# A graph layer and its experts: products and low parts by blocks of columns, one-hots with a scalar operand, high parts behind both layers

## The chip, the cores and the metric

The kernel runs on one core of a Trainium2 chip. The time is the device time of one execution in microseconds (us), as the median of three runs. Every number of the profile comes from one further, profiled execution.

## The reference

x is 6250 rows of 256 numbers, with 100,000 edges sorted by their target dst. Layernorm is LN(x). The kernel computes

```
h    = LN(x);  r = relation_emb[edge_type];  gate = sigmoid(r @ gate_w.T + gate_b)
m    = (clifford(h[src] * r, msg_w, msg_b)) * gate * (deg_src[src] * deg_dst[dst]) ** -0.5
x    = x + clifford(h + segment_sum(m, dst), upd_w, upd_b)
w    = softmax(mean(LN(x)) @ Wr + br)          # per row here: the leading axis has length 1
x    = x + sum over 8 experts e of w[:, e] * (relu(bn2(relu(bn1(LN(x) @ W1[e])) @ W2[e])) @ Wo[e] + bo[e])
```

where clifford is a 256x256 matrix put together from four 64x64 parts.

## The kernel before

Edges come in blocks of 128 (one a partition), four blocks to a superblock; there are 196 superblocks. Rows of x come in 49 tiles of 128, in 27 groups of one or two tiles (22 have two). A group of two tiles uses up 8 superblocks.

*A superblock J.* GpSimd gathers its four blocks of 260 columns of the scaled h table into H (L440, one indirect DMA a block; a ring of 6 superblocks), and the relation rows of two or three of the blocks into R. The other one or two blocks' relation rows are read by TensorE instead: ScalarE makes a one-hot of the edge type (L571, L574) and TensorE multiplies it with the relation table into PSUM (`rel_pe`, L885). VectorE then makes the products in place: H times R over all gathered blocks in one instruction (L1287, 520 or 780 columns; 1040 in the last superblocks) and H times PSUM for each block that was read (L1291, 258 columns). Columns 256 and 257 carry the norm and a one; columns 258 and 259 are padding.

TensorE sums the products over the edges of a target by a one-hot S of the edge's place in its tile. It does so in a reduced format, and so each product is split: ScalarE makes the high part HI (`high_act`, L583, 1040 columns), VectorE the low part LO = H - HI (`low_dve`, L1304, 1040 columns) and S for four blocks in one instruction (L1300, two broadcast operands). TensorE multiplies S with HI and LO (`sb_pe`, L873). VectorE takes the sums out of PSUM for each two superblocks (`take_dve`, L1262, L1266).

*A group g* runs its experts in ten stages s0 to s9 (`ffn` of each engine). In stage s TensorE does layer w1 of expert s, layer w2 of expert s-1 (both L825) and the output y of expert s-2 (L857); ScalarE the two relus (L632) into h1 and h2; VectorE adds y into acc (L1238). So s8 has no w1, s9 only y, s0 only w1. At the end of a stage comes its hook, with the work of the next groups in an order written out by hand: one superblock in each of s0 to s3, s5, s6, s8 and s9, and none in s4 and s7; in s1 the normed rows of the next group are transposed (L767, which waits for ScalarE's relu to free its PSUM slot), in s4 its sums (L792, copied to aT by ScalarE, L586), in s5 they are multiplied (L801), in s7 the rows for the experts (L767) and in s8 the router (L813). z has two PSUM slots, each used by the layers and the transposes in turn.

In the hook for superblock J VectorE does take(J), S and LO of J+1, the products of J+2; TensorE reads the relation rows of J+2, for which the products up to J+1 must be done (their PSUM slots are used again), then sums J. ScalarE makes the one-hots of the types of J+3 and puts the high part of J+2 on a list; `rest()` works the list off, and is called between the two relu layers of the next stage.

Ahead of all this a start-up of some 125 us counts degrees, scales h and stores the tables. GpSimd's queue then issues gathers one after another; for superblock J from 6 on it waits until LO of J-5 is done (L440 is the helper's line).

Of the kernel before, what the change touches and what calls it, by code (L numbers as in the profile page):

```python
# [7 lines left out]
P = 128  # L8
D = 256
DX = 260  # L10
NE = 8
SB = 4
SE = SB * P
NH = 6
# [69 lines left out]
def build(nc, a, out, n, e, nrel):  # L84
# [31 lines left out]
    with ctx:  # L116
# [211 lines left out]
        with nc.Block() as block:  # L328
# [165 lines left out]
            def _(act):  # L494
# [93 lines left out]
                def program(z):  # L588
                    def full():
                        i, no = z.next()  # L590
                        act.wait_ge(z_full, no)
                        return z_at(i)

                    def norm_act(g):
                        t0, nt = GROUPS[g]
                        act.wait_ge(x_ld[g % 3], 16 * (g // 3 + 1))
                        for t in range(nt):
                            last = s_.activation(hgA[:, t, :], acc[:, g % 3, t, :], ACT.Identity,
                                                 bias=nmr[:, t0 + t:t0 + t + 1], scale=rstd[:, t0 + t:t0 + t + 1])
                        last.then_inc(hx_ready, 1)  # L600

                    def hx_act(g):
                        z_ = full()
                        copy(hxT[:, :, 0:wide[g]], z_[:, :, 0:wide[g]]).then_inc(z_free, 1)

                    def at_act(g):
                        t0, nt = GROUPS[g]
                        for t in range(nt):
                            z_ = full()
                            copy(aT[:, t, :, :], z_[:, :, 0:P]).then_inc(z_free, 1)  # L610
                        act.wait_ge(dd_in, g + 1)
                        s_.activation(dd[:, 0:nt], dd[:, 0:nt], ACT.Sqrt).then_inc(dd_sd, 1)

                    def var_act(g):
                        t0, nt = GROUPS[g]
                        act.wait_ge(var_in, g + 1)
                        s_.activation(rs[:, 0:nt], rs[:, 0:nt], ACT.Sqrt).then_inc(var_sd, 1)

                    def ht_act(g):
                        z_ = full()  # L620
                        copy(hT[:, :, 0:wide[g]], z_[:, :, 0:wide[g]]).then_inc(z_free, 1)

                    def soft_act(g):
                        t0, nt = GROUPS[g]
                        act.wait_ge(sm_in, g + 1)
                        s_.activation(lg[:, 0:nt, :], lg[:, 0:nt, :], ACT.Exp).then_inc(sm_exp, 1)

                    def layer(l, e_, o, wide_):
                        z_ = full()
                        for m in range(2):  # L630
                            c = e_ * 2 + m
                            last = s_.activation(o[:, m, 0:wide_], z_[:, m, 0:wide_], ACT.Relu,  # L632
                                                 bias=bns[:, l, 1, c:c + 1], scale=bns[:, l, 0, c:c + 1])
                        last.then_inc(z_free, 1)

                    def ffn(g, hook, between):
                        for s in range(NE + 2):
                            if s < NE:
                                layer(0, s, h1[:, s % 2, :, :], wide[g])
                            between()  # L640
                            if 0 < s <= NE:
                                layer(1, s - 1, h2[:, (s - 1) % 2, :, :], wide[g])
                            hook(f"s{s}")

                    return norm_act, hx_act, at_act, var_act, ht_act, soft_act, ffn

                def fast():
                    norm_act, hx_act, at_act, var_act, ht_act, soft_act, ffn = program(Ring(ZS))
                    norm_act(0)
                    types_act(0)  # L650
                    types_act(1)
                    hx_act(0)
                    types_act(2)
                    high_act(0)
                    high_act(1)
                    waiting = []

                    def sb_act(some, later):

                        for J in some:  # L660
                            rest()
                            types_act(J + 3)
                            waiting.append(J + 2)
                        if not later:
                            rest()

                    def rest():
                        while waiting:
                            high_act(waiting.pop(0))

                    sb_act(range(END[0]), False)
                    at_act(0)
                    late = shares(1, 0) if NG > 1 else [()] * 4
                    for i in range(4):
                        if i == 1:
                            var_act(0)
                        if i == 2:
                            ht_act(0)
                        if i == 3:
                            soft_act(0)  # L680
                        sb_act(late[i], i == 3)
                    for g in range(NG):
                        early = shares(g + 1, 1) if g + 1 < NG else None
                        late = shares(g + 2, 0) if g + 2 < NG else None

                        def hook(p):
                            if g + 1 == NG:
                                return
                            if p == "s6":
                                var_act(g + 1)  # L690
                            if p in EARLY:
                                sb_act(early[EARLY.index(p)], True)
                            if p in LATE and late:
                                sb_act(late[LATE.index(p)], True)
                            if p == "s0":
                                norm_act(g + 1)
                            if p == "s1":
                                hx_act(g + 1)
                            if p == "s4":
                                at_act(g + 1)  # L700
                            if p == "s7":
                                ht_act(g + 1)
                            if p == "s8":
                                soft_act(g + 1)

                        ffn(g, hook, rest)

                def general():
                    norm_act, hx_act, at_act, var_act, ht_act, soft_act, ffn = program(Ring(ZS))
                    act.sem_inc(oh_t, NQ)  # L710
                    act.wait_ge(w2_out, 1)
                    zero()
                    for g in range(NG):
                        norm_act(g)
                        hx_act(g)
                        if g + 1 < NG:
                            act.wait_ge(at_ready, g + 1)
                            zero()
                        at_act(g)
                        var_act(g)  # L720
                        ht_act(g)
                        soft_act(g)
                        ffn(g, lambda p: None, lambda: None)

                act.wait_ge(nm_ready, 1)
                branches(act, fast, general)
# [256 lines left out]
            def _(dve):  # L983
# [296 lines left out]
                def prod_dve(J):  # L1280

                    if J >= NSB:
                        return
                    dve.wait_ge(gr[J % NR], gathered(J))
                    dve.wait_ge(gh[J % NH], 64 * (J // NH + 1))
                    cut = PLACE[J][1] * DX
                    last = v.tensor_tensor(H[:, J % NH, 0:cut], H[:, J % NH, 0:cut], rows(J), ALU.mult)  # L1287
                    for q, b in read_blocks(J, WHOLE):
                        dve.wait_ge(rel_full, q + 1)
                        h_ = H[:, J % NH, b * DX:b * DX + D + 2]  # L1290
                        last = v.tensor_tensor(h_, h_, PR[:, q % 2, 0:D + 2], ALU.mult)  # L1291
                    last.then_inc(prod, 1)

                def low_dve(J):
# [2 lines left out]
                        return  # L1297
                    if J > 1:
                        dve.wait_ge(mm, J - 1)
                    v.tensor_tensor(S[:, J % 2, :, :], dloc[:, J * SB:(J + 1) * SB].unsqueeze(2).to_broadcast([P, SB, P]),  # L1300
                                    iota_w[:, 0:P].unsqueeze(1).to_broadcast([P, SB, P]), ALU.is_equal)
                    dve.wait_ge(hi_ready, J + 1)
                    h_ = H[:, J % NH, :]
                    v.tensor_tensor(LO[:, J % 2, :], h_, HI[:, J % 2, :].bitcast(fp32), ALU.subtract).then_inc(lo_ready, 1)  # L1304

                def sb_dve(some):
                    for J in some:
# [142 lines left out]
```

## Time and profile before

| what | value |
|---|---|
| median of 3 runs | 1969.0 us (1965.43 to 1970.19) |
| profiled execution, its own time | 1968.44 us |
| its span, first to last instruction | 1966.5 us |
| TensorE matmuls busy | 1799.6 us, 92% of the span, 10653 instructions |
| VectorE busy | 1146.0 us, 58%, 2344 instructions |
| ScalarE busy | 1311.2 us, 67%, 2943 instructions |
| GpSimd busy | 1411.6 us, 72%, 1413 instructions |
| mean granted TensorE clock | 0.979 of full speed |

In the profile PE is TensorE's matmuls, PEld its weight loads, DVE VectorE, ACT ScalarE, POOL GpSimd. L12 is line 12 of the kernel. An instruction's time runs from its start to its end; on one engine neighbours overlap by some hundredths of a us, so what an instruction costs its engine is the time from its start to the next one's start. A time in brackets is the engine's idle time ahead, with what ended it.

### The profile page before, as it was taken

How to read it: one execution, taken by the hardware profiler on the slowest of the kernel's cores; microseconds unless marked ns; L12 is line 12 of the kernel's file. 1: busy time of each engine (PE TensorE's matmuls, PEld its weight loads, DVE VectorE, ACT ScalarE, POOL GpSimd, SP SyncE). 2: the span in 40 equal slices, each digit the busy share in tenths (PEclk: the TensorE clock that was granted, in tenths of full speed). 3: DMA queues.
4: the chain of work that ended last, by engine and by line, in shares of the span. 5: the costliest groups of instructions: out<-in, count | busy, mean ns of one | idle time of the engine just before them, and what ended most of it. 6: DMA issues, size and time to landing. Idle time of an engine off the chain costs nothing.

```text
span 1966.5 us, 31036 instructions
## 1 busy us (share of the span) xinstructions
PE 1799.6 (92%) x10653; PEld 1591.6 (81%) x10653; DVE 1146.0 (58%) x2344; ACT 1311.2 (67%) x2943; POOL 1411.6 (72%) x1413
## 2 busy tenths in 40 slices
PE   6835898999999999999999999999999999999988
PEld 5825887888888888888888888888888888888878
DVE  8965665655555645655655655655565565555442
ACT  5455786766767767767767767767767766774455
POOL 4867777777777777777777777777777677777500
PEclk9967999999999999999999999999999999999999
DMA  8176344434434434434434434434444443433300
GB/s 234 52 268 195 98 119 120 125 99 122 125 99 124 124 100 124 123 100 124 123 98 124 124 97 125 124 99 120 121 109 110 114 120 100 120 106 101 74 12 6
DMA packets 87319, 226.32 MB, mean 115 GB/s; under 512 B 23261, under 2 KB 37723, under 8 KB 87216
## 3 DMA queue, kind: packets, MB, share of 16 engines
q0 software_dynamic: 61872, 171.67, 33.0%
q1 hardware_dynamic: 24528, 52.36, 8.6%
q10 hardware_dynamic: 815, 1.16, 0.2%
q8 instruction: 34, 0.56, 0.1%
q14 instruction: 70, 0.57, 0.1%
HBM read 211.66 MB, written 13.44 MB: 114 GB/s over the span
## 4 chain that ended last, share of the span: by engine, by line
PE 68%; DVE 9%; POOL 8%; ACT 7%; issue 7%; DMA 1%; DVEq 0%; POOLq 0%; ACTq 0%; SPq 0%
PE z L825 29%; PE y L857 15%; PE pr L885 10%; PE o L873 6%; POOL H L440 6%; ACT OH L571 2%; POOL R L440 2%; PE y L782 2%; DVE H L1011 2%; ACT h L632 2%; DVE acc L1238 2%; PE y L735 2%; DVE LO L1304 1%; PE y L801 1%; ACT HI L583 1%
## 5 line engine op out<-in xcount | busy, mean ns | idle before, releaser
L440 POOL DMA_INDIRECT H<-h_table,src x784 | 829.2, 1058 | 264.2 <-issue 243.5
L632 ACT ACTIVATE h<-z,bns 128x256 f32<-128x256 f32 (+1 forms) x864 | 421.6, 540 | 475.8 <-PE z L825 474.4
L440 POOL DMA_INDIRECT R<-r_table,typ x505 | 565.1, 1119 | 171.2 <-issue 170.9
L1238 DVE SCALAR_TENSOR_TENSOR acc<-y,wg,acc 128x256 f32<-128x256 f32 x392 | 173.4, 480 | 563.5 <-PE y L857 563.3
L825 PE MATMUL z<-hT,big 128*128 128x256 f32 (+1 forms) x1728 | 379.9, 363 | 9.3 <-ACT aT L586 5.1
L825 PE MATMUL z<-h,big 128*128 128x256 f32 (+1 forms) x1728 | 376.7, 361 | 3.8 <-ACT h L632 1.9
L857 PE MATMUL y<-big,h 128*128 128x256 f32 x1568 | 377.1, 381 | 1.7 <-DVE lg L1201 1.6
L885 PE MATMUL pr<-RH,OH 125*128 125x258 f32 x1116 | 310.5, 312 | 52.6 <-DVE H L1291 40.3
L571 ACT ACTIVATE OH<-tb,iota_t 125x128 fp32r<-125x128 int32 x1116 | 353.9, 393 | 0.0
L825 PEld LDWEIGHTS z<-h,big 128*128 128x128 f32 x1728 | 305.6, 191 | 41.1 <-ACT h L632 3.9
L825 PEld LDWEIGHTS z<-hT,big 128*128 128x128 f32 x1728 | 296.0, 191 | 44.5 <-ACT aT L586 9.9
L857 PEld LDWEIGHTS y<-big,h 128*128 128x128 f32 x1568 | 291.6, 190 | 42.1 <-issue 1.9
L885 PE MATMUL pr<-RL,OH 125*128 125x258 f32 x1116 | 286.2, 290 | 0.0
L885 PEld LDWEIGHTS pr<-RH,OH 125*128 125x128 f32 x1116 | 219.7, 197 | 76.3 <-DVE H L1291 37.6
L1304 DVE TENSOR_TENSOR LO<-H,HI 128x1040 fp32r<-128x1040 f32 x196 | 242.3, 1236 | 50.5 <-ACT HI L583 50.4
L583 ACT ACTIVATE HI<-H 128x1040 fp32r<-128x1040 f32 x196 | 208.9, 1066 | 49.7 <-DVE H L1291 42.7
L885 PEld LDWEIGHTS pr<-RL,OH 125*128 125x128 f32 x1116 | 220.3, 197 | 1.9
L873 PE MATMUL o<-HI,S 128*128 128x258 f32 x784 | 202.5, 289 | 1.0 <-DVE LO L1304 1.0
L873 PE MATMUL o<-LO,S 128*128 128x258 f32 x784 | 200.3, 286 | 0.0
L1287 DVE TENSOR_TENSOR H<-H,R 128x780 f32<-128x780 f32 (+1 forms) x196 | 166.5, 849 | 48.2 <-DMA H<-h_table,src 48.2
L574 ACT ACTIVATE OH<-OH 125x512 fp32r<-125x512 f32 x279 | 176.2, 632 | 8.8
L873 PEld LDWEIGHTS o<-HI,S 128*128 128x128 f32 x784 | 152.4, 194 | 1.6 <-DVE LO L1304 1.2
(177 smaller groups left out, 1584.3 us busy)
## 6 DMA issues: line engine op xcount, KB each, us to landing
tb<-in_typ_row SPq DMA_DIRECT2D x24, 672.0 KB
H<-h_table,src POOLq DMA_INDIRECT x784, 2.8
R<-r_table,typ POOLq DMA_INDIRECT x505, 2.8
h_table<-big SPq DMA_DIRECT2D x7, 910.0 KB, 8.7
big<-in_x SPq DMA_DIRECT2D x7, 896.0 KB, 10.9
big<-in_w SPq DMA_DIRECT2D x8, 768.0 KB, 4.9
acc<-in_x SPq DMA_DIRECT2D x22, 256.0 KB, 6.5
out<-acc SPq DMA_DIRECT2D x22, 256.0 KB
```

The lines of the kernel that those rows point to most:

```text
L440: pool.indirect_dma_start(out=to[:, b * DX:(b + 1) * DX], out_offset=None, in_=tab, in_offset=bass.IndirectOffsetOnAxis(ap=ix[:, J * SB + ...
L571: last = s_.activation(OH[:, q % 3, k, :], tb[:, c % 2, at_:at_ + P], ACT.Abs, bias=iota_t[:, k:k + 1])
L574: s_.activation(OH[:, q % 3, :, :], OH[:, q % 3, :, :].bitcast(fp32), ACT.Relu, scale=-1.0, bias=1.0).then_inc(oh_t, 1)
L583: s_.activation(HI[:, J % 2, :], H[:, J % NH, :], ACT.Copy).then_inc(hi_ready, 1)
L632: last = s_.activation(o[:, m, 0:wide_], z_[:, m, 0:wide_], ACT.Relu, bias=bns[:, l, 1, c:c + 1], scale=bns[:, l, 0, c:c + 1])
L825: last = pe.matmul(o[:, m, 0:N], wt[:, e_, k, m * P:(m + 1) * P], x[:, k, 0:N], start=k == 0, stop=k == 1)
L857: last = pe.matmul(o[:, t * D:(t + 1) * D], h2[:, e_ % 2, k, t * P:(t + 1) * P], wo[:, e_, k, :], start=k == 0, stop=k == 1)
L873: last = pe.matmul(O[:, j // 2 % 2, 0:D + 2], S[:, j % 2, b, :], x[:, j % 2, b * DX:b * DX + D + 2], start=j % 2 == b == 0 and x is HI, st ...
L885: last = pe.matmul(PR[:, q % 2, 0:D + 2], OH[:, q % 3, k, :], x[:, k, 0:D + 2], start=k == 0 and x is RH, stop=k == 3 and x is RL)
L1238: last = v.scalar_tensor_tensor(out=acc[:, g % 3, t, :], in0=b[:, t * D:(t + 1) * D], scalar=wg[:, t, e_:e_ + 1], in1=acc[:, g % 3, t, :], ...
L1287: last = v.tensor_tensor(H[:, J % NH, 0:cut], H[:, J % NH, 0:cut], rows(J), ALU.mult)
L1304: v.tensor_tensor(LO[:, J % 2, :], h_, HI[:, J % 2, :].bitcast(fp32), ALU.subtract).then_inc(lo_ready, 1)
```

## The change

The products H times R and the low parts H - HI are made one block of 258 columns at a time in place of one instruction over all blocks with the padding. The one-hots S are made a block at a time, by a comparison of the row of numbers 0 to 127 with one per-partition scalar, in place of a comparison of two broadcast operands. And ScalarE calls `rest()` at the beginning of the hook, behind both relu layers, in place of between them.

```diff
-                    def ffn(g, hook, between):
+                    def ffn(g, hook):
                         for s in range(NE + 2):
                             if s < NE:
                                 layer(0, s, h1[:, s % 2, :, :], wide[g])
-                            between()
                             if 0 < s <= NE:
                                 layer(1, s - 1, h2[:, (s - 1) % 2, :, :], wide[g])
                             hook(f"s{s}")
...
                         def hook(p):
+                            rest()
                             if g + 1 == NG:
                                 return
...
-                        ffn(g, hook, rest)
+                        ffn(g, hook)
...
-                    cut = PLACE[J][1] * DX
-                    last = v.tensor_tensor(H[:, J % NH, 0:cut], H[:, J % NH, 0:cut], rows(J), ALU.mult)
+                    for b in range(PLACE[J][1]):
+                        h_ = H[:, J % NH, b * DX:b * DX + D + 2]
+                        last = v.tensor_tensor(h_, h_, rows(J)[:, b * DX:b * DX + D + 2], ALU.mult)
...
-                    v.tensor_tensor(S[:, J % 2, :, :], dloc[:, J * SB:(J + 1) * SB].unsqueeze(2).to_broadcast([P, SB, P]),
-                                    iota_w[:, 0:P].unsqueeze(1).to_broadcast([P, SB, P]), ALU.is_equal)
+                    for b in range(SB):
+                        v.tensor_scalar(S[:, J % 2, b, :], iota_w[:, 0:P], dloc[:, J * SB + b:J * SB + b + 1], None, ALU.is_equal)
                     dve.wait_ge(hi_ready, J + 1)
-                    h_ = H[:, J % NH, :]
-                    v.tensor_tensor(LO[:, J % 2, :], h_, HI[:, J % 2, :].bitcast(fp32), ALU.subtract).then_inc(lo_ready, 1)
+                    for b in range(SB):
+                        c = slice(b * DX, b * DX + D + 2)
+                        last = v.tensor_tensor(LO[:, J % 2, c], H[:, J % NH, c], HI[:, J % 2, c].bitcast(fp32), ALU.subtract)
+                    last.then_inc(lo_ready, 1)
```

## Rows read from the trace of the kernel before

**Rows 1.** Busy time by stretch: span, PE, PEld, DVE, ACT, POOL (instructions), clock, DMA, GB/s.

```profile
125.00:380.00 255.00, 201.63 (x1245) 182.89 (x1246) 147.07 (x311) 176.72 (x408) 197.66 (x183) 0.90 0.48 135
380.00:1760.00 1380.00, 1325.31 (x7504) 1165.53 (x7503) 793.91 (x1677) 965.03 (x2114) 1056.85 (x1002) 1.00 0.43 115
...
457.90:464.60 6.70, 6.70 (x29) 6.01 (x28) 2.08 (x3) 4.06 (x10) 5.46 (x5) 0.63 0.68 192
```

**Rows 2.** Waits of TensorE from 378 to 1757: total us, times, longest.

```profile
PE z L767 <- ACT h L632: 30.1, 19, 1.7
PE pr L885 <- DVE H L1291: 13.6, 20, 0.7
...
PE z L825 <- issue: 2.6, 1, 2.6
```

**Rows 3.** Timeline of TensorE, s9 to s1 of one group: start, us, what, [idle before].

```profile
1031.23 1.89 PE L857 MATMUL y<-big,h 128*128 128x256 f32 x8
1033.80 0.39 PE L885 MATMUL pr<-RH,OH 125*128 125x258 f32 x1 [0.68 <-DVE H L1291]
...
1036.78 1.89 PE L825 MATMUL z<-hT,big 128*128 128x256 f32 x8
1038.80 0.39 PE L885 MATMUL pr<-RH,OH 125*128 125x258 f32 x1
...
1046.30 0.66 PE L767 MATMUL z<-ident,hgA 128*128 128x128 f32 x4 [1.60 <-ACT h L632]
...
1106.09 0.39 PE L885 MATMUL pr<-RH,OH 125*128 125x258 f32 x1 [0.68 <-DVE H L1291]
```

**Rows 4.** Timeline of VectorE, the superblocks of s8 and s9 there.

```profile
1030.70 0.68 DVE L1300 TENSOR_TENSOR S<-dloc,iota_w 128x512 fp32r<-128x512 f32 x1
1031.30 1.23 DVE L1304 TENSOR_TENSOR LO<-H,HI 128x1040 fp32r<-128x1040 f32 x1
1032.45 0.96 DVE L1287 TENSOR_TENSOR H<-H,R 128x780 f32<-128x780 f32 x1
1033.33 0.41 DVE L1291 TENSOR_TENSOR H<-H,pr 128x258 f32<-128x258 f32 x1
...
1037.39 0.69 DVE L1287 TENSOR_TENSOR H<-H,R 128x520 f32<-128x520 f32 x1
1038.00 0.75 DVE L1291 TENSOR_TENSOR H<-H,pr 128x258 f32<-128x258 f32 x2
```

**Rows 5.** Timeline of VectorE: instructions with scalar operands elsewhere.

```profile
102.82 9.22 DVE L1056 TENSOR_SCALAR big<-big,hgB 128x256 f32<-128x256 f32 x28
...
122.01 0.33 DVE L1089 TENSOR_SCALAR masks<-sums 128x98 f32<-128x98 f32 x2
...
1017.65 0.88 DVE L1194 TENSOR_SCALAR hgB<-acc,mv,rs 128x256 f32<-128x256 f32 x2
```

**Rows 6.** Timeline of ScalarE in s4.

```profile
1071.03 1.06 ACT L583 ACTIVATE HI<-H 128x1040 fp32r<-128x1040 f32 x1
1071.99 1.02 ACT L632 ACTIVATE h<-z,bns 128x256 f32<-128x256 f32 x2
1073.79 0.66 ACT L586 ACTIVATE aT<-z 128x256 f32<-128x256 f32 x2 [0.78 <-PE z L792]
```

**Rows 7.** Timeline of TensorE in front: two long stalls.

```profile
176.08 0.55 PE L885 MATMUL pr<-RH,OH 125*128 125x258 f32 x1 [6.74 <-DVE H L1291]
...
309.67 0.58 PE L885 MATMUL pr<-RH,OH 125*128 125x258 f32 x1 [4.40 <-DVE H L1291]
```

**Rows 8.** Timeline of GpSimd: gathers, free and held.

```profile
146.07 4.71 POOL L440 DMA_INDIRECT H<-h_table,src  x1 [0.30 <-issue]
...
1007.65 0.95 POOL L440 DMA_INDIRECT H<-h_table,src  x1 [0.30 <-issue]
1008.91 1.98 POOL L440 DMA_INDIRECT R<-r_table,typ  x1 [0.30 <-issue]
```

**Rows 9.** The gathers alone, by stretch: span, busy (instructions), clock, DMA, GB/s.

```profile
125.00:309.00 184.00, 142.51 (x131) 0.87 0.52 148
```

More of the change, by code:

```diff
@@ L722, in general @@
                         soft_act(g)
-                        ffn(g, lambda p: None, lambda: None)
+                        ffn(g, lambda p: None)
                 act.wait_ge(nm_ready, 1)
```

## The prediction

> **What bounds the kernel now.** Read the stretches first [rows 1]: from 380 to 1760 TensorE is busy for 1325.31 of 1380 us, 96%, at full granted clock. Ahead of it, from 125 to 380, it is busy for 201.63 of 255 at a granted clock of 0.90. So most of the time is TensorE's own work, which the change doesn't touch; it can move only what TensorE waits for. Next, who it waits for in the long middle [rows 2]: in nineteen groups the first transpose of the next group's rows (L767) waits 1.6 us for ScalarE's relu, twenty times the read matmuls (L885) wait 0.68 us for VectorE's products, and once it waits 2.6 us at the loop's entry.
>
> The timeline of one group shows the place of both [rows 3]. In stage s9 the y matmuls end at 1033.12, and the relation reads, which want the products of the next superblock, start at 1033.80. In s0 w1 ends at 1038.67 and the reads start at 1038.80. In s1 the transpose waits 1.60 us. The group repeats after 1106.09 - 1033.80 = 72.29 us. VectorE's timeline [rows 4] says why: from the end of y in s8 it has no idle time: accumulation, router logits, two takes, one-hots S (1030.70), low parts LO (1031.30), products with R (1032.45), product with PSUM (1033.33), ended 0.06 us before TensorE starts. Anything longer in this run is waited for. Elsewhere in a group VectorE waits for TensorE before each accumulation, up to 5 us, so longer superblocks are hidden there: the products of s2 to s6 end more than 3 us before their readers start.
>
> The front is another matter: there the gathers are late. TensorE's long stalls at 176.08 and 309.67 (6.74 and 4.40 us) end with a product [rows 7], a third of 1.51 us follows at 318.80, and each of these products began only when VectorE had waited some 5 us for the gathered h rows.
>
> **The change part by part.** All durations are of one execution whose span is 1966.5 us, in a run of 1968.44 us; the median of the three runs is 1969.0, 0.6 above it.
>
> *Blocks of 258 for LO and products.* What counts is the step from start to start. LO of 1040 elements takes 1032.45 - 1031.30 = 1.15 us, the product of 780 takes 1033.33 - 1032.45 = 0.88, that of 520 takes 1038.00 - 1037.39 = 0.61 [rows 4]. The line through them is 1.04 ns an element and 0.07 us an instruction, so a block of 258 takes 0.34. Four make 1.35 for LO (+0.20), three 1.01 (+0.13), two 0.67 (+0.06). The product with PSUM, 258 wide, has just this step (two in 0.75), so the line holds there.
>
> *One-hots with a scalar operand.* Today 0.60 us (1031.30 - 1030.70). The row nearest in kind is the scaling of x, TENSOR_SCALAR with per-partition scalars, 28 of 256 elements in 9.22 us, 0.33 each [rows 5]. Taking off 128 elements at 1.04 leaves 0.19, four of them 0.76: +0.16. That is one element a cycle. Lower end: the masks (98 elements, immediate operand) take two in 0.33 us, a step near 0.12, which is two elements a cycle; at that pace four blocks take 0.49, -0.11. Upper end: hgB, two instructions with pointers in 0.88, a step of 0.40 to 0.45 per 256, or 0.26 per 128: 1.04, +0.44. I take +0.16, since the first row has pointer, SBUF source and float32 like the new one.
>
> The Trainium skill (VectorE: DVE Perf Modes, The perf-mode tier table) gives tensor_scalar in float32 from SBUF two elements a cycle, without excepting pointer operands. This trace has 0.33 us for 256 with pointers, one a cycle. By the page the one-hots would become cheaper, and that is a rival below.
>
> Sum for the run in s8: 0.16 + 0.20 + 0.13 = 0.49 us. In s9: 0.16 + 0.20 + 0.06 = 0.42. The reads of s9 start 0.49 later, those of s0 0.91 later in all; but the transpose in s1 hangs on ScalarE's queue, which starts with the relu after w1 of s0 and so moves by 0.49 only, and takes up the 0.42 out of its 1.60. So 0.49 a group. Twenty groups have this wait [rows 2], and the two narrow ones in front have it too: 22 x 0.49 = +10.7. Bounds: 22 x 0.22 = +4.8 and 22 x 0.77 = +17. In the tail the last superblocks stand in the same places, with products of four blocks: +1.
>
> *High parts behind both layers.* HI takes 0.96 us from start to start on ScalarE. In s8, s9 and s0 only one relu layer or none stands in the stage, and HI keeps its place, so the 1.60 us wait in s1, which comes of what ScalarE does in s0, stays. In s1 to s7 the second layer's relu now waits only for TensorE and HI comes up to 1.8 us later; its reader LO comes later still except in s1 (LO at 1.0 later, hidden: next reads are 7 us off). In s4 the copy of aT is on TensorE's path. Today relu, HI, relu, then aT at 1073.79 when the transposes end [rows 6]. Afterwards the second relu starts at 1071.85 when w2 is done, ends its step at 1072.76, HI at 1073.72: 0.07 us in hand. Cost 0; if that cover goes, up to 0.9 in each of 20 groups (+18), and up to 0.5 won where late products hold ScalarE in front. I take 0.
>
> *GpSimd.* A gather takes 0.95 us and the next starts 0.30 later [rows 8]. One that starts during a VectorE instruction with two SBUF operands is held: at 1008.91 the gather starts with LO (1008.83 to 1010.07) and takes 1.98; LO's end plus the usual rest is its end. At 146.07 it takes 4.71, through four such instructions in a row [rows 8]. From 125 to 309, 131 gathers are busy for 142.51 us [rows 9], 18 us more than 131 x 0.95. The delay goes with the square of the length of the holding instructions: for two superblocks today 2(0.68² + 1.23²) + 0.96² + 0.69² = 5.3; after, thirteen blocks of 0.42 give 2.3, if the scalar one-hots (one SBUF stream) hold nothing. So some 10 of the 18 us go. Where does it count? (a) The gathers at 142 to 152 are 5 us late and the pipeline's first superblocks stand on them; VectorE's own work then comes last for one of them, weights' loads share the DMA: gain 4.5, bounds 1 and 5.5. (b) By 309 the gathers are 10 us earlier while their users moved by 4.5 less 1: the stalls of 4.40 and 1.51 go: gain 6, bounds 0 and 7.5 (a stall so long may cost clock behind it, too). (c) From 380 on no stall comes of a gather [rows 2]: nothing.
>
> The Trainium skill (SBUF — State Buffer, SBUF: two separate sides) says that VectorE holds the shared ports also in a two-port mode with a single source. In this trace only the holding by two-operand instructions is seen. If the one-hots ran in that mode, their short steps would hold too, and the 2.3 would be 2.9, 2 us less won in front.
>
> Sum: +10.7 + 1 - 4.5 - 6 = +1.2 us, 1969.6 by the profiled run, 1970.2 by the median.
>
> **Rivals.**
> (1) *The gathers gain nothing.* Place: 125 to 320. A held gather must get in between two blocks; eight to twelve blocks now follow one another, and at 146.07 one was let in only when VectorE paused. If that is the rule and not the exception, the gain is 2 rather than 10.5: +10, 1979. For it: that row. Against: at 1008.91 it got in at LO's end with the product right behind. It decides if gathers over 2 us become common.
> (2) *Pointer operand dear*: 0.26 a block, +0.28 x 22 = +6, 1976. The second hgB speaks for it, the 28 in a row against.
> (3) *One-hots at two elements a cycle*: -0.27 x 22 = -6, 1964. The immediate masks speak for it, pointer rows against.
> (4) *The move reaches s1*: if HI left ScalarE's queue ahead of the relu that s1's transpose waits for, 0.96 x 20 = -19, 1951. By the order of the queue it doesn't.
> (5) *The clock.* The 2.6 us wait at the loop's entry is followed by a granted clock of 0.63 over 457.9 to 464.6, half speed for most of it [rows 1, 2], some 2 us lost. If stages s9 to s1, with idle 2.9 in place of 2.4, bring that each group: +40, 2010. Against: the longest single wait gets shorter, 1.2.
>
> **How the numbers follow.** Forecast 0.48, (1) 0.15, (2) 0.10, (3) 0.13, (4) 0.08, (5) 0.06. A measurement of this kernel tells about 0.3% (5.9 us) from no change. Faster: (4), over half of (3), and 0.09 from the forecast's own range of 1962 to 1976: 0.25. Slower: (1), (5), and 0.06 of (2) and the forecast: 0.27. Same: 0.48. The range leaves out (4) and (5): 1957 to 1983.
>
> **What would show it.** The waits of L885 for VectorE in the middle at 1.2 us in s9 and a new one near 0.5 in s0, L767's at 1.2, period 72.8; one-hot steps of 0.19; gathers at mean 1.00 in front, no stall over 3 us near 310; VectorE some 90 us busier. Wrong: a period at or under 72.3, one-hots at 0.12, or aT's wait above 0.3.

## The result, and the profile after

The kernel after took 1977.5 us (median of seven runs, 1973.3 to 1983.5) against 1969.0 of before: ratio 1.0048, 95% interval [1.0031, 1.0065]. It is slower, by more than a measurement of this kernel leaves open. The forecast was 1970.2, range 1957 to 1983. A second measurement (the last experiment) gave 1.0064 [1.0041, 1.0087]. Three executions of the experiments count as slow and are left out of the ratios: one of alternate (2330.8 us at a granted clock of 0.756) and two of late blocks (1968.3 and 1970.4 us).

The profiled execution has a span of 1975.6 us, 9.1 above that of before. First the page's busy times; VectorE has 94 us more (1240.2).

```profile
PE 1800.0 (91%) x10653; PEld 1592.4 (81%) x10653; DVE 1240.2 (63%) x3829; ACT 1322.9 (67%) x2943; POOL 1448.2 (73%) x1413
```

The stretches of [rows 1], same columns. GpSimd's instructions of the middle take 1.09 us on average, where they took 1.05.

```profile
125.00:380.00 255.00, 203.28 (x1234) 184.47 (x1234) 158.83 (x529) 176.94 (x405) 197.99 (x183) 0.88 0.47 135
380.00:1760.00 1380.00, 1317.14 (x7467) 1158.19 (x7467) 860.96 (x2801) 970.03 (x2104) 1078.77 (x990) 1.00 0.42 113
```

TensorE's waits in the middle, beside [rows 2]. VectorE's products are now waited for 38 times, not 20; the transposes wait less; the wait at the loop's entry is not there.

```profile
PE pr L885 <- DVE H L1292: 33.9, 38, 1.2
PE z L767 <- ACT h L632: 22.1, 19, 1.2
PE z L825 <- ACT aT L586: 4.8, 19, 0.3
```

One group of TensorE, beside [rows 3]: the wait in s9 is 1.19, there is one of 0.59 in s0, and that of s1 shrank from 1.60 to 1.17.

```profile
1036.57 0.39 PE L885 MATMUL pr<-RH,OH 125*128 125x258 f32 x1 [1.19 <-DVE H L1292]
1042.02 0.39 PE L885 MATMUL pr<-RH,OH 125*128 125x258 f32 x1 [0.59 <-DVE H L1292]
1049.04 0.66 PE L767 MATMUL z<-ident,hgA 128*128 128x128 f32 x4 [1.17 <-ACT h L632]
1076.94 1.99 PE L825 MATMUL z<-hT,big 128*128 128x256 f32 x8 [0.25 <-ACT aT L586]
```

VectorE there, beside [rows 4]. From start to start, the four one-hots take 0.79 (0.60 before), the low parts 1.35 (1.15), three products 1.01 (0.88).

```profile
1032.95 0.86 DVE L1302 TENSOR_SCALAR S<-iota_w,dloc 128x128 fp32r<-128x128 f32 x4
1033.74 1.43 DVE L1306 TENSOR_TENSOR LO<-H,HI 128x258 fp32r<-128x258 f32 x4
1035.09 1.09 DVE L1288 TENSOR_TENSOR H<-H,R 128x258 f32<-128x258 f32 x3
1036.10 0.42 DVE L1292 TENSOR_TENSOR H<-H,pr 128x258 f32<-128x258 f32 x1
```

GpSimd in the same stretch, and a gather of the front, beside [rows 8]. The gather at 1034.74 starts in the third block of the low parts and isn't let in at that block's end, nor at the next three: its end less the usual 0.85 us is 1036.15, where the last product with R ends (1035.09 + 1.09).

```profile
1033.42 1.01 POOL L440 DMA_INDIRECT R<-r_table,typ  x1 [0.30 <-issue]
1034.74 2.26 POOL L440 DMA_INDIRECT R<-r_table,typ  x1 [0.30 <-issue]
...
149.55 2.52 POOL L440 DMA_INDIRECT H<-h_table,src  x1 [0.30 <-issue]
```

The gathers alone in front, beside [rows 9]: no fewer microseconds, and one gather less in the same time.

```profile
125.00:309.00 184.00, 143.13 (x130) 0.85 0.51 145
```

TensorE's stalls there, beside [rows 7]. The first is 3 us shorter, but two near 310 stand (3.06 and 4.86), where the prediction wanted none over 3.

```profile
170.72 0.36 PE L885 MATMUL pr<-RH,OH 125*128 125x258 f32 x1 [3.73 <-DVE H L1292]
...
265.11 0.36 PE L885 MATMUL pr<-RH,OH 125*128 125x258 f32 x1 [2.74 <-DVE H L1292]
274.42 1.11 PE L792 MATMUL z<-ident,sums 128*128 128x128 f32 x4 [3.54 <-DVEq L1278]
301.87 0.55 PE L885 MATMUL pr<-RH,OH 125*128 125x258 f32 x1 [3.06 <-DVE H L1292]
312.89 0.58 PE L885 MATMUL pr<-RH,OH 125*128 125x258 f32 x1 [4.86 <-DVE H L1292]
```

Between the first stall and these lies a turn. In s9 of a front group around 240 us TensorE is 8.2 us ahead of the kernel before, and at the reads around 301 it is 1.4 behind (301.87, where before has 300.43). The first line is of before, the second of after.

```profile
243.74 0.36 PE L885 MATMUL pr<-RH,OH 125*128 125x258 f32 x1 [1.68 <-DVE H L1291]
```

```profile
235.56 0.36 PE L885 MATMUL pr<-RH,OH 125*128 125x258 f32 x1 [2.19 <-DVE H L1292]
```

To see where the 9.1 us lie, take the start of the reads in s9 of the first and the last of twenty regular groups (378.67 and 1756.70 before, 381.37 and 1764.56 after). **Front** +2.7; **middle** 1383.19 against 1378.03, +5.2; **tail** 211.0 against 209.8, +1.2. The middle has nineteen periods: each is 72.8 now (median 72.79) where it was 72.28, +9.8 in all; and in before one was 76.91, that with the 2.60 us wait at the loop's entry, which this execution lacks: -4.6.

### The profile page after: what moved, and what is told of

It is laid out like the page before. It is cut to its first block, busy times and chain, and to the rows that moved or that the text cites. A ratio compares the mean times of both kernels' runs of the same rounds, so it can differ in the third digit from the quotient of the medians.

```text
span 1975.6 us, 32521 instructions
## 1 busy us (share of the span) xinstructions
PE 1800.0 (91%) x10653; PEld 1592.4 (81%) x10653; DVE 1240.2 (63%) x3829; ACT 1322.9 (67%) x2943; POOL 1448.2 (73%) x1413
## 4 chain that ended last, share of the span: by engine, by line
PE 68%; DVE 11%; ACT 9%; POOL 6%; issue 6%; DMA 1%; DVEq 0%; ACTq 0%
PE z L825 29%; PE y L857 13%; PE pr L885 11%; PE o L873 7%; POOL H L440 4%; ACT OH L571 3%; ACT HI L583 2%; PE y L782 2%; DVE H L1011 2%; ACT h L632 2%; POOL R L440 2%; DVE LO L1306 2%; DVE acc L1238 2%; PE y L735 2%; PE y L801 1%
## 5 line engine op out<-in xcount | busy, mean ns | idle before, releaser
L440 POOL DMA_INDIRECT H<-h_table,src x784 | 852.4, 1087 | 245.8 <-issue 244.6
L440 POOL DMA_INDIRECT R<-r_table,typ x505 | 579.1, 1147 | 171.2 <-issue 167.0
L1306 DVE TENSOR_TENSOR LO<-H,HI 128x258 fp32r<-128x258 f32 x784 | 281.1, 420 | 41.6 <-ACT HI L583 41.6
L1288 DVE TENSOR_TENSOR H<-H,R 128x258 f32<-128x258 f32 x505 | 186.8, 420 | 39.4 <-DMA H<-h_table,src 39.4
L873 PE MATMUL o<-HI,S 128*128 128x258 f32 x784 | 203.0, 289 | 1.2 <-DVE LO L1306 1.2
L873 PE MATMUL o<-LO,S 128*128 128x258 f32 x784 | 200.9, 287 | 0.0
L1302 DVE TENSOR_SCALAR S<-iota_w,dloc 128x128 fp32r<-128x128 f32 x784 | 173.0, 297 | 0.0
```

Source lines behind the costliest of these rows:

```text
L440: pool.indirect_dma_start(out=to[:, b * DX:(b + 1) * DX], out_offset=None, in_=tab, in_offset=bass.IndirectOffsetOnAxis(ap=ix[:, J * SB + ...
L873: last = pe.matmul(O[:, j // 2 % 2, 0:D + 2], S[:, j % 2, b, :], x[:, j % 2, b * DX:b * DX + D + 2], start=j % 2 == b == 0 and x is HI, st ...
L1288: last = v.tensor_tensor(h_, h_, rows(J)[:, b * DX:b * DX + D + 2], ALU.mult)
L1306: last = v.tensor_tensor(LO[:, J % 2, c], H[:, J % NH, c], HI[:, J % 2, c].bitcast(fp32), ALU.subtract)
```

## Experiments

Three readings are given for each run. The **period** is the median of those nineteen. The **front** is the start of the first regular group's s9. The **excess** is the time of the gathers above 0.947 us each (a free one), summed from 125 us on, and up to 309 us in brackets. "Later" counts gathers held past the end of the VectorE instruction that ran 0.05 us behind their start; in after, all 91 gathers over 2 us are such. "Entries" are waits at the loop's entry. Each row is one profiled execution; the ratio to before comes from unprofiled runs too.

| kernel | period | front | excess | later | entries | ratio [95%] |
|---|---|---|---|---|---|---|
| before | 72.28 | 378.7 | 143 (19.3) | 4 | 1 | 1 |
| after | 72.79 | 381.4 | 182 (20.2) | 102 | 0 | 1.0048 [1.0031, 1.0065] |
| after again | 72.77 | 382.3 | 173 (21.1) | 100 | 1 | 1.0064 [1.0041, 1.0087] |
| high parts between | 72.77 | 380.3 | 176 (18.6) | 98 | 0 | 1.0072 [1.0047, 1.0097] |
| broadcast one-hots | 72.60 | 372.7 | 117 (14.4) | 37 | 4 | 1.0001 [0.9977, 1.0024] |
| blocks undone | 72.45 | 380.6 | 148 (18.3) | 83 | 1 | 1.0027 [1.0003, 1.0050] |
| alternate | 72.77 | 380.0 | 139 (19.6) | 153 | 2 | 1.0033 [1.0010, 1.0057] |
| gate last | 72.76 | 378.7 | 199 (17.8) | 103 | 3 | 1.0098 [1.0071, 1.0124] |
| gate first | 72.78 | 381.7 | 175 (21.1) | 108 | 1 | 1.0065 [1.0040, 1.0090] |
| four broadcasts | 72.86 | 379.7 | 212 (18.9) | 104 | 3 | 1.0095 [1.0070, 1.0121] |
| late takes | 72.13 | 372.5 | 97 (12.4) | 40 | 2 | 0.9993 [0.9961, 1.0026] |
| late places | 71.31 | 370.8 | 105 (13.4) | 4 | 0 | 0.9848 [0.9821, 0.9875] |
| late scalar | 71.3 | 373.4 | 108 (12.9) | 3 | 9 | 0.9875 [0.9838, 0.9912] |
| late blocks | 71.41 | 372.8 | 74 (12.4) | 22 | 0 | 0.9885 [0.9850, 0.9920] |

(For late scalar the period is that of groups without a wait at the entry.)

**High parts between: the move undone.** The kernel after, where `ffn` calls `rest()` between the two layers again.

```diff
-                    def ffn(g, hook):
+                    def ffn(g, hook, between):
...
+                            between()
...
-                            rest()
```

> The kernel after, with the high parts put back between the two relu layers; blocks and scalar one-hots stay. Theory T (the loss is VectorE's longer run in s8, +0.49 us a group, and gathers that stay held to the end of a run of adjacent two-operand VectorE instructions; the place of the high parts is worth nothing): 1977 us within 3, period 72.8, waits of L885 1.2 and 0.6 us, excess of held gathers (time above 947 ns each, after 125 us) 180 us within 15. Rival A (the high parts behind both layers delay something in front or in s4): 3 us or more below the kernel after, with aT's wait or a wait in front shorter.

1982.2 us (1979.1 to 1991.3). Period, front and excess are those of after, and the ratio's interval overlaps that of after. Rival A's gain of 3 us isn't there; the move costs and gives nothing that these runs can tell.

**Broadcast one-hots: the scalar form undone.**

```diff
-                    for b in range(SB):
-                        v.tensor_scalar(S[:, J % 2, b, :], iota_w[:, 0:P], dloc[:, J * SB + b:J * SB + b + 1], None, ALU.is_equal)
+                    v.tensor_tensor(S[:, J % 2, :, :], ... to_broadcast([P, SB, P]), ... ALU.is_equal)
```

> The kernel after, with the four scalar one-hots again one instruction on two broadcast operands (0.60 us in place of 0.78). T: the period falls by 0.18 us to 72.6, but this instruction holds gathers as the others do, and makes the run of holding instructions one longer: excess 215 us (200 to 235), which costs some of the 3.5 us back in front; total 1975 to 1979, and the same whatever the order of the two effects. Rival R (gathers are slower because VectorE has more instructions, holding or not): four instructions become one, so the excess falls below 170 us and the total to 1972.

1970.5 us. The period is as expected, 72.60, but T's excess (215) is far off: 117, and the front is 8.7 us earlier. So blocks of low parts and products, with one wide one-hot instruction ahead, mostly let the gathers in, as the prediction had wanted (37 are still held later), and 135 gathers fit ahead of 309 us, where before has 131 and after 130.

```profile
125.00:309.00 184.00, 141.70 (x135) 0.82 0.52 152
```

**Blocks undone: the scalar one-hots alone.**

```diff
-                    for b in range(SB):
-                        c = slice(b * DX, b * DX + D + 2)
-                        last = v.tensor_tensor(LO[:, J % 2, c], ...)
+                    v.tensor_tensor(LO[:, J % 2, :], h_, HI[:, J % 2, :].bitcast(fp32), ALU.subtract).then_inc(lo_ready, 1)
```

(and the products whole again.)

> The kernel after, with the low parts and the products whole again; scalar one-hots and the place of the high parts stay. T: the one-hots no longer hold a gather, and a gather held by a whole LO gets in at its end: excess 115 us (100 to 135; the kernel before has 141, the kernel after 180). The period is that of before + 0.16 to 0.20 = 72.45; total 1970 (1966 to 1972). Rival R (the scalar one-hots are to blame for the slower gathers): the excess stays at 170 or more, and the front stays as late as in the kernel after.

1975.6 us, 1.0027. Both theories miss: the excess is 148, between the two. Its parts tell more. In before, every gather that is held by the whole LO gets in at LO's end [rows 8]; here, of 124 that are held by it, 80 don't. VectorE and GpSimd at one such place: the gather starts 0.42 us before LO ends and gets in at 1032.57, at the product's end.

```profile
1029.70 0.86 DVE L1301 TENSOR_SCALAR S<-iota_w,dloc 128x128 fp32r<-128x128 f32 x4
1030.49 1.23 DVE L1304 TENSOR_TENSOR LO<-H,HI 128x1040 fp32r<-128x1040 f32 x1
1031.64 0.96 DVE L1287 TENSOR_TENSOR H<-H,R 128x780 f32<-128x780 f32 x1
```

```profile
1031.30 2.12 POOL L440 DMA_INDIRECT H<-h_table,src  x1 [0.30 <-issue]
```

Nothing in LO or the product was changed against before; only what stands ahead of them was.

**Alternate: one-hot 0, low part 0, one-hot 1, ...**

```diff
                     for b in range(SB):
                         c = slice(b * DX, b * DX + D + 2)
+                        v.tensor_scalar(S[:, J % 2, b, :], iota_w[:, 0:P], dloc[:, J * SB + b:J * SB + b + 1], None, ALU.is_equal)
                         last = v.tensor_tensor(LO[:, J % 2, c], ...)
```

> The kernel after, with the one-hot blocks and the low-part blocks in turn (one-hot 0, low part 0, one-hot 1, low part 1, ...), same instructions, same count, same VectorE time. T: each one-hot is an instruction that holds nothing between two that do, so that a gather gets in after one block of 0.33 us: excess 80 us or less (the three product blocks still stand together, so not zero), first regular group some 5 to 9 us earlier, total 1966 to 1972 with the period still 72.8. Rival R (number of instructions): excess 180 us or more, total 1977 as the kernel after. Rival Q (the gather waits for the run of all VectorE instructions, whatever their operands): excess 200 us or more.

1976.4 us, 1.0033. The excess fell to 139 but not to 80, the front didn't move, and more gathers are held past their instruction than in after (153 for 102, though by 0.76 us on average where after has 1.55). T falls: it isn't enough that a one-hot stands between two instructions that hold. Of 113 gathers that start in a one-hot here, 52 are held, with a low part 0.2 us behind each one-hot; of 108 in after, 15 are, 14 of them by 0.1 us at most.

**Gate last and gate first: two scalar, one broadcast, in both orders.**

```diff
-                    for b in range(SB):
+                    for b in (0, 1):
                         v.tensor_scalar(S[:, J % 2, b, :], ...)
+                    v.tensor_tensor(S[:, J % 2, 2:4, :], dloc[...].unsqueeze(2).to_broadcast([P, 2, P]), iota_w[...]..., ALU.is_equal)
```

(in the other kernel the broadcast instruction makes one-hots 0 and 1 and comes first.)

> The kernel after, with one-hots 0 and 1 by the scalar form and one-hots 2 and 3 by one instruction on broadcast operands, in this order, so that a holding instruction stands directly ahead of the low parts; everything else as after. Both theories: period 72.74 (one-hots 0.73 us in place of 0.78). Theory G (the broadcast one-hot is a gate: a gather that starts in it or ahead of it is let in at its end, and so starts its next one late in the run, where it gets in too): excess of gathers after 125 us near that of the kernel with broadcast one-hots, 110 to 135 us, first regular group at 373 to 377 us, total 1971 to 1974. Theory C (scalar one-hots do harm by their number): excess half way between 117 and 182, 150 us, here and with the other order.

> The same six instructions as in the other kernel of this pair in the other order: one instruction on broadcast operands for one-hots 0 and 1, then one-hots 2 and 3 by the scalar form, then the low parts. G: no holding instruction stands directly ahead of the low parts, so gathers start anywhere in their blocks as in the kernel after: excess 165 to 190 us, first regular group at 380 us or later, total 1976. C: excess 150 us as with the other order, no difference in front.

1989.6 and 1981.1 us; excess 199 and 175; 103 and 108 gathers held later. G wanted a large drop with the first order, C 150 with both. Both fall: with the one-hots in three parts the whole harm is there, in either order.

**Four broadcasts: short one-hots, but not scalar ones.**

```diff
-                        v.tensor_scalar(S[:, J % 2, b, :], iota_w[:, 0:P], dloc[:, J * SB + b:J * SB + b + 1], None, ALU.is_equal)
+                        v.tensor_tensor(S[:, J % 2, b, :], dloc[:, J * SB + b:J * SB + b + 1].to_broadcast([P, P]), iota_w[:, 0:P], ALU.is_equal)
```

> The kernel after, with each of the four one-hots made by a TENSOR_TENSOR on the broadcast place and the row of numbers in place of the scalar form: same count, same size, and by the line through VectorE's steps (0.07 us and 1.04 ns an element) the same step of 0.20 us; only the form differs. Both theories: period 72.8. Theory F (it is the scalar form ahead of the low parts that leaves gathers held through the whole run): excess after 125 us 130 us or less, first regular group at 371 to 376 us, total 1966 to 1972. Theory P (what counts is when the parts of the run fall, not their form): excess 165 us or more, first regular group at 379 or later, total 1975 to 1980.

1988.9 us, 1.0095; excess 212, 104 held later. F falls and P stands: it isn't the scalar form. The same 0.20 us steps by another instruction do the same, and somewhat more, since these hold gathers themselves.

```profile
1032.54 0.88 DVE L1302 TENSOR_TENSOR S<-dloc,iota_w 128x128 fp32r<-128x128 f32 x4
1033.35 1.43 DVE L1306 TENSOR_TENSOR LO<-H,HI 128x258 fp32r<-128x258 f32 x4
```

**Late takes: the take of the sums behind the products** (broadcast one-hots, blocks).

```diff
-                        take_dve(J)
                         low_dve(J + 1)
                         prod_dve(J + 2)
+                        take_dve(J)
```

> The kernel after with broadcast one-hots, and on VectorE the take of the sums (0.79 us in s8) behind the products in place of ahead of the one-hots. By the timeline of before: one-hots 0.60, low parts 1.35 and products 1.01 from 1029.91 on put the last product's start at 1032.87, and TensorE starts 0.47 behind that, 0.22 us after its y matmuls end in place of 0.68. Period 72.28 - 0.46 = 71.8 (0.8 below the kernel with broadcast one-hots), wait of L885 0.2 in s9 and about 1 us in s0, that of L767 near 0.55. Front as with broadcast one-hots (373). Total 1955 (1950 to 1962). Rival: the take is waited for by TensorE (it frees the accumulators O), and a new wait at L873 gives back half or more: total over 1962.

The profiled execution took 1961.3 us, with the wait of s9 as worked out, those of s0 and s1 longer (1.18 and 0.81, where about 1 and 0.55 were expected), a front of 372.5 and a period of 72.13. That is 0.47 below the broadcast one-hots, where 0.8 was expected:

```profile
1021.86 0.39 PE L885 MATMUL pr<-RH,OH 125*128 125x258 f32 x1 [0.22 <-DVE H L1292]
1027.90 0.39 PE L885 MATMUL pr<-RH,OH 125*128 125x258 f32 x1 [1.18 <-DVE H L1292]
1034.56 0.66 PE L767 MATMUL z<-ident,hgA 128*128 128x128 f32 x4 [0.81 <-ACT h L632]
```

But the median of twelve executions is 1973.2, from 1956.3 to 1983.5. No new wait at L873 is in the trace, so the rival isn't shown; what makes one execution 20 us longer than another is taken up below.

**Late places: low parts and products first, one-hots and take behind them** (before, with whole parts).

```diff
                     for J in some:
-                        take_dve(J)
-                        low_dve(J + 1)
-                        prod_dve(J + 2)
+                        low_dve(J + 1)      # LO only
+                        prod_dve(J + 2)
+                        place_dve(J + 1)    # S, gives lo_ready
+                        take_dve(J)
```

> The kernel before, with whole low parts and products first, and the one-hots and the take of the sums behind them on VectorE. By the timeline of before the products of s8 end 1.4 us earlier and TensorE's wait of 0.68 in s9 goes: period 71.6. G: nothing stands ahead of the low parts as a gate, so a gather that starts in them often stays held through the product: excess 145 to 165 us as with scalar one-hots and whole low parts (148), first regular group at 378 to 381. Total 1956 (1951 to 1962). C: no scalar one-hots, so the excess is that of the kernel before, 143 us or less.

1938.3 us (1933.7 to 1946.4): 0.9848, the fastest of all. VectorE's run in s8 now has its last product at 1012.08, and TensorE goes from its y matmuls into the reads of s9 at 1012.91 with no wait; 0.48 us are left in s0.

```profile
1010.04 1.24 DVE L1302 TENSOR_TENSOR LO<-H,HI 128x1040 fp32r<-128x1040 f32 x1
1011.20 0.96 DVE L1287 TENSOR_TENSOR H<-H,R 128x780 f32<-128x780 f32 x1
1012.08 0.42 DVE L1291 TENSOR_TENSOR H<-H,pr 128x258 f32<-128x258 f32 x1
1012.41 0.69 DVE L1308 TENSOR_TENSOR S<-dloc,iota_w 128x512 fp32r<-128x512 f32 x1
```

```profile
1011.37 1.89 PE L857 MATMUL y<-big,h 128*128 128x256 f32 x8
1012.91 0.47 PE L885 MATMUL pr<-RH,OH 125*128 125x258 f32 x1
...
1018.34 0.39 PE L885 MATMUL pr<-RH,OH 125*128 125x258 f32 x1 [0.48 <-DVE H L1291]
...
1025.48 0.66 PE L767 MATMUL z<-ident,hgA 128*128 128x128 f32 x4 [1.29 <-ACT h L632]
```

```profile
PE z L767 <- ACT h L632: 23.5, 20, 1.3
PE pr L885 <- DVE H L1291: 11.0, 19, 0.8
```

The period fell by 0.97, not 0.68. From the first of the eight y matmuls to the first read it is 1.54 us here (1011.37 to 1012.91) and 2.57 in before [rows 3]: a read that needn't wait starts ahead of the modelled end of the matmul before it, so a removed wait gives back more than its idle time. Most of what s0 waits more (0.48), s1 waits less (1.29 for 1.60). The front came 7.9 us earlier and the excess is 105, which is against G too: it wanted 145 to 165, as no gate stands ahead of LO, and the gathers get in.

**Late scalar** (late places, `S` again by four `tensor_scalar`) and **late blocks** (late places, `LO` and products by blocks).

> The kernel with low parts and products first and the places late, with its one-hots by the scalar form (0.78 in place of 0.60 us). No wait of s9 hangs on them; that of s0 grows by 0.18 and that of the transposes shrinks by it: period 71.3 as with broadcast one-hots there. F, if the scalar form does harm only directly ahead of the low parts: excess 115 us or less, first regular group at 371, total 1938. F, if it does harm wherever it stands: excess 140 us or more, first regular group 377 or later, total 1945 to 1950.

> The kernel with low parts and products first and the places late, with low parts and products block by block. VectorE's run in s8 gets 0.33 us longer, which just fits ahead of the end of TensorE's y matmuls (by the trace with whole parts, 1012.08 + 0.33 + 0.47 against 1012.91): wait in s9 0 to 0.1, in s0 1.06, of the transposes 0.7; period 71.3 to 71.4. If blocks without scalar one-hots let gathers in earlier, as in the kernel with broadcast one-hots: excess 80 to 105 us, first regular group at 370, total 1938 (1934 to 1942). If block borders hold gathers whatever stands ahead: excess 140 us or more, first regular group at 377, total 1945.

Late scalar: 3 gathers held later, excess 108: behind the products, split one-hots do no harm to the gathers. Late blocks: excess 74, the least of all, and 1940.6 us (1937.4 to 1970.4). So block borders as such don't hold gathers, and here the blocks do what they were credited with. But the gathers aren't what the middle waits for, and the blocks lengthen the run that is: the total isn't below that of late places.

Late scalar's time, 1949.4 us from 1936.0 to 1964.6, shows another thing. TensorE's loop holds two groups; at the head of each of nine rounds its profiled execution has a wait that no engine or queue ends. The waits of the middle, and the first:

```profile
PE z L825 <- issue: 18.7, 9, 2.4
```

```profile
450.24 2.64 PE L825 MATMUL z<-hT,big 128*128 128x256 f32 x8 [2.28 <-issue]
```

The nine groups with it take 73.4 to 75.4 us where the others take 71.3: 2.1 to 4.1 each, 28 in all; this execution took 1964.6 us, 28.6 more than the fastest of its kernel. Before has it once in its profile, after not at all.

**After again.**

> The kernel after, unchanged, on the chip of this call: how far one profiled execution of the same program stands for others. If the excess of held gathers and the front belong to the program: excess 175 to 187 us, first regular group at 380 to 382.5 us, period 72.8, ratio to before 1.003 to 1.007. If they are chance: excess or front as different from the first trace (181.6, 381.4) as the kernel with broadcast one-hots is (116.8, 372.7).

1980.6 us; excess 173 (2 under the range), 100 held later, front 382.3. The slow gathers and the late front belong to the program, not to one execution.

## Why the prediction was right in range and 7 us too low

**The middle: right.** Steps, waits and period came out as worked out: one-hots 0.79 for four (0.76 expected), LO 1.35, products 1.01; waits 1.19, 0.59, 1.17; period 72.8. The Trainium skill (VectorE: DVE Perf Modes, The perf-mode tier table) would have the scalar one-hots at two elements a cycle; the trace has a step of 0.20 us for 128, one a cycle, and rivals (2) and (3) fall with it. (The price of rival (3) was worked out for 98 elements: 128 at two a cycle would be 0.07 + 0.07 us, four of them 0.55 and not 0.49.) The two halves add up: blocks undone +0.17 a period over before, broadcast one-hots +0.32, both together +0.51.

**The high parts: right.** Cost 0; aT's wait stayed at 0.25, and undoing the move changed nothing. Rival (4) falls.

**The tail**: +1.2 against +1, which is luck: the second profile of after has a tail of 208.4 us, 2.6 less than the first.

**GpSimd: the step that failed.** The prediction took 10.5 us off the front "if the scalar one-hots (one SBUF stream) hold nothing". Where they stand together they hold almost nothing: of 108 gathers that start in one, 93 are free. But the delay of the others didn't go "with the square of the length of the holding instructions". That rule needs every held gather to get in at the end of the instruction that holds it. In before 270 of 274 do; in after 102 of 277 stay past it, 97 of them until the last product with R ends, 1.55 us each, and they give 158 of the 182 us of excess. So the front, where 9.0 us were to be won (10.5 less three waits of 0.49), lost 2.7: 11.7 off. Before has one profile, and after has 381.4 and 382.3 in two, so that the loss is less sure than the missing gain.

Of the two terms, the first, (a), came: by 240 us TensorE was 8.2 ahead, with 4.5 forecast. The second, (b), failed: "by 309 the gathers are 10 us earlier" would be eight gathers more at 1.25 us each, and there was one less (130 for 131). GpSimd's queue ran no faster over the front. The lead was used up in waits for gathers: VectorE waits 2.44, 2.67 and 4.04 us for h rows at 253.77, 263.52 and 272.08, and before has no such wait between 250 and 300.

```profile
272.08 0.77 DVE L1288 TENSOR_TENSOR H<-H,R 128x258 f32<-128x258 f32 x2 [4.04 <-DMA H<-h_table,src]
```

In the middle, where nineteen periods of +0.49 were to lose 9.3, 5.2 were lost, as the wait at the loop's entry which the profile of before happened to have wasn't there: 4.1 the other way, by luck. Front, middle and tail (0.2) make 7.8 of the 7.9 us between 1967.7, the span that the sum gives, and 1975.6.

Rival (1), with a chance of 0.15, had the right test (gathers over 2 us: 7 before, 91 after) and the right size, 1979. The gathers are let in at the end of the run, as it said; its reason, many blocks in a row, is not the right one. The runs separate it:

- one wide one-hot instruction ahead: whole parts 4 held later, blocks 37
- one-hots split in three or four, all directly ahead: whole parts 83, blocks 98 to 108
- one-hots behind the products, wide or split: whole parts 4 and 3, blocks 22

It is the split of the one-hots ahead of the low parts that does most of it, whatever their form; blocks add 15 to 33 in each line. Why a gather is passed over at a border then, and not otherwise, stays open: the time left to the border doesn't tell (in after, of 23 gathers that start 264 to 296 ns ahead of the end of the second block of low parts, 18 get in there and 5 don't). That a wide instruction in the one-hots' last place suffices was tried and is false.

**What the excess is worth** the fourteen profiles show: the front goes with the excess up to 309 us. The five with 12.4 to 14.4 have the first regular group at 370.8 to 373.4, the nine with 17.8 to 21.1 at 378.7 to 382.3; the slope is 1.2 us a microsecond, the correlation 0.96. It is mainly that between the two sets (0.77 within the nine, none within the five), so it shows which kernels have the late front, not a price for each microsecond. The start of the reads behind the start-up scatters between 131.2 and 134.0 on its own, and hardly carries through. In the middle the excess costs nothing, as term (c) had it: with 212 us the period is 72.86, with 175 it is 72.78. Yet the two kernels with the most excess, gate last and four broadcasts, have the highest ratios (1.0098 and 1.0095). Their profiles have three entries each, which cost their middles 12 to 13 us; whether the excess brings on entries isn't shown. With the broadcast one-hots the excess in front is 4.9 us less and the front 6.0 earlier, 7.0 with three waits of 0.32 added back. That is two thirds of the 10.5: with most gathers let in, the size was still too large.

**Rival (5) falls.** With idle 2.95 us from s9 to s1 in each group, the granted clock of the middle is 1.00 as in before. The wait at the loop's entry, from which the rival was argued, is there 0 and 1 times in after's two profiles, and most often (9 times) in a kernel with shorter waits. Whether this wait makes the 20 us steps between executions of late takes and late blocks (1937.4 to 1941.4 and then 1961.1 to 1970.4) is likely by its size (nine make 28) and not shown, as only one execution of each has a trace.

## What to carry to other kernels

Where a shared resource is granted at the borders of another engine's instructions, shorter instructions don't by themselves mean shorter waits: count in the trace at which border the waiting one got in, and look at what precedes the run. Price each added instruction at its fixed step (0.07 us here) on the run that another engine waits for, and look first at the order of that run: moving what nobody waits for behind what is waited for gave 1.5%, where cutting the run into shorter instructions lost 0.5%. A single profile can hold or lack an event worth 5 us; compare periods, and count such events apart.

## What the runs showed of the hardware

- TENSOR_SCALAR with a pointer, float32 in SBUF, 128 elements: step 0.20 us, the same as TENSOR_TENSOR on a broadcast operand of that size. Four in a row leave 93 of 108 gathers that start in them free; with a low part behind each (alternate) 52 of 113 are held.
- A gather can be passed over at up to seven borders of VectorE instructions in after (up to twelve in four broadcasts). The Trainium skill (SBUF — State Buffer, SBUF: two separate sides) has the pair of ports held "for the whole instruction" by whichever starts first; it doesn't say who is next. Here a waiting gather often wasn't (102 of 277), and lost 0.7 to 2.5 us, where the step of one block is 0.34.
- TensorE's wait at a loop's head, 1.8 to 3.1 us: 0 to 9 times a profile, depending on the kernel and the execution. With what follows it costs the group 2 to 5 us.
